# The router's keys as three products of split parts, with the splits on GpSimd

## The chip, the core and the metric

The kernel runs on one core of one Trainium2 chip. The core has five engines that run side by side, each its own list of instructions in order, and that wait for one another through semaphores: TensorE (PE, with its weight loads shown apart as PEld), VectorE (DVE), ScalarE (ACT), GpSimd (POOL) and SyncE (SP), which here issues DMAs. The metric is the device time of one execution in microseconds; a time is the median of several runs.

## The reference, cut to what matters

Thirty-two sequences of 128 tokens with 128 channels pass through a transformer block (self attention with 16 heads, cross attention to a context, a gelu MLP) and then through a block of routed experts. The change touches one product of the second block:

```python
nx = layer_norm(x, ln_gamma, ln_beta)              # 128 tokens x 128 channels, each sequence
q = nx @ Wq
k = prototype_bank @ Wk                            # prototype_bank is the context
scores = einsum('bth,bph->btp', q, k) * H ** -0.5
weights = softmax(scores)
evidence = weights @ (prototype_bank @ Wv)
combined = concat([nx, evidence, anchor])
router_probs = softmax(combined @ router_W + router_b)
h = silu(combined @ e_w1[e] + e_b1[e])             # three experts, 256 wide each
routed = sum over e of (h @ e_w2[e] + e_b2[e]) * router_probs[e]
g = sigmoid(silu(combined @ gate_w1 + gate_b1) @ gate_w2 + gate_b2)
out = x + g * (routed @ out_w + out_b)
```

## The kernel before, in words

The 32 sequences are worked in 8 groups of 4, so a group's tile is 128 partitions by 512 columns. The first 320 us or so are attention. Near their end the kernel derives matrices from the weights; one is `A`, the product of `Wk` and `Wq` (line 965, copied out of PSUM at line 779), so that the scores need one product per group, `A` with the transposed context (`keys`, line 1031), and one with the normalised tokens (`scores`).

The MLP of the 8 groups follows, and the router and experts after that. The order of the work there is written out by hand: `MLP_STEPS` (line 383) and `ROUTER_STEPS` (line 391) list steps as (name, how many groups ahead, part), and `rest_of_groups` (line 418) walks the lists. Every engine walks the same lists and emits what it has for a step, so a step's place in the list is its place in each engine's queue. Router steps of the first two groups are spread between the last MLP steps (lines 425 to 432); the first iteration over `ROUTER_STEPS` is unrolled, four run in a loop (line 446), and three more are unrolled.

An iteration of the router begins with the seven `hidden` products of group i and ends with its four `expert` products. In between stand the steps for the two groups ahead: statistics and normalisation, keys, transposition, scores and softmax for group i+2, and the evidence of group i+1.

Names that the prediction uses:

- `keys`: TensorE multiplies `A` with `CTXT`, the transposed context of one group, both float32, into a PSUM bank; VectorE copies the bank to `KEYS` (line 869).
- `hidden`: six products per chunk, of operands that are split in two parts of type float32r, the value rounded (high) and what rounding left (low): high by high, high by low, low by high, for the tokens (`NXS` with `WNS`) and for the evidence (`EVS` with `US`).
- `split` (line 663) is the GpSimd helper that makes such parts: one tensor-tensor instruction adds zeros to the source and writes the high part, and after a semaphore a second one subtracts that from the source and writes the low part. It runs for `EVS` (step `evidence`) and for `NXS` (step `nx_read`).
- `expert` for each of four sequences: TensorE makes three products side by side; VectorE adds the bias (`T`, line 933), multiplies the first third by its probability (`R`, line 936), and adds the other two in two more instructions (line 939, each waits for the one before it). TensorE has two banks for this, so the product for sequence b waits until VectorE has read that for b-2 (line 1089).
- Between expert 0 and expert 1 VectorE has the steps `scores` (lines 880 to 887) and `gate` (line 926).
- `stats` and `norm` are row statistics and normalisation (lines 814 to 828), with the inverse deviation from GpSimd (lines 655, 657).
- SyncE loads a group's context (`CTX`) and transposed context (`CTXT`, one buffer for all groups); the load of `CTXT` waits for the keys of the group before (line 631).

Of the kernel before, what the change touches and what calls it, by code (L numbers as in the profile page):

```python
# [25 lines left out]
P = 128  # L26
# [187 lines left out]
def round_steps(i):  # L214
    if i == -1:
        steps = first_steps()
    elif i == 0:
        steps = [e for e in regular_steps(0) if e[2] not in ("xt_s", "proj_s", "yt_s", "v1")]
        steps += (fill_steps(0.2, "xt_s", 2, (0, 0.3), (1, 2.1))
                  + stats_steps(3.2, 4.2, "ln_s", 3) + norm_steps(5.0, "ln_s", 3)  # L220
                  + fill_steps(14.0, "xt_s", 3, (0, 14.1), (1, 15.1))
                  + fill_steps(27.0, "proj_s", 0, (0, 27.1), (1, 27.2)) + fill_steps(30.0, "yt_s", 0, (1, 30.1))
                  + [(20.1, "load", "weights", 0, 0)])
    elif i in (1, 2):
        steps = [e for e in regular_steps(i) if i == 2 or e[2] not in ("proj_s", "yt_s")]
        steps += (fill_steps(10.0, "proj_s", 2 * i - 1, (0, 10.1), (1, 10.2))
                  + fill_steps(12.0, "yt_s", 2 * i - 1, (1, 12.1)))
        if i == 1:
            steps += (fill_steps(27.0, "proj_s", 2, (0, 27.1), (1, 27.2)) + fill_steps(30.0, "yt_s", 2, (1, 30.1))
                      + [(4.1, "load", "weights", 1, 0), (20.1, "load", "weights", 2, 0)])  # L230
    elif i == NG - 3:
        steps = (crossed_steps(i) + early_statistics(i) + fill_steps(27.0, "proj_s", NG - 1, (0, 27.1), (1, 27.2))
                 + fill_steps(30.0, "yt_s", NG - 1, (1, 30.1)))
    elif i == NG - 2:
        steps = (crossed_steps(i) + fill_steps(27.0, "proj_c", NG - 4, (1, 27.1))
                 + fill_steps(29.0, "yt_c", NG - 4, (1, 29.1)))
    elif i == NG - 1:
        steps = (fill_steps(3.0, "v1", i, (1, 3.1))
                 + fill_steps(8.0, "proj_c", NG - 3, (1, 8.1)) + fill_steps(10.0, "yt_c", NG - 3, (1, 10.1))
                 + fill_steps(12.0, "derive", 0, (0, 12.1), (1, 12.1), (2, 12.2))  # L240
                 + fill_steps(15.0, "derive", 1, (0, 15.1)) + fill_steps(17.0, "derive", 2, (0, 17.1))
                 + fill_steps(19.0, "derive", 3, (0, 19.1)) + fill_steps(21.0, "derive", 4, (0, 21.1))
                 + fill_steps(23.0, "derive", 5, (0, 23.1)) + fill_steps(25.0, "derive", 6, (0, 25.1))
                 + fill_steps(27.0, "proj_c", NG - 2, (1, 27.1)) + fill_steps(29.0, "yt_c", NG - 2, (1, 29.1))
                 + fill_steps(31.0, "mlp_xt", 0, (0, 31.1))
                 + [(t, "split", "weights", k, 0) for k, t in enumerate((2.5, 6.0, 9.0, 22.5, 24.5))]
                 + mlp_steps(21.2, "stats", 0) + mlp_steps(23.4, "norm", 0)
                 + mlp_steps(25.5, "stats", 1))
    elif i == NG:
        steps = (mlp_steps(0.2, "norm", 1)  # L250
                 + mlp_steps(2.0, "first", 0, 0) + mlp_steps(2.1, "first", 0, 1) + mlp_steps(2.6, "stats", 2)
                 + mlp_steps(3.0, "xt", 1) + mlp_steps(5.0, "first", 0, 2) + mlp_steps(5.1, "xt_read", 1)
                 + mlp_steps(7.0, "first", 0, 3) + mlp_steps(8.0, "gelu", 0, 2) + mlp_steps(8.01, "second", 0, 0)
                 + fill_steps(8.1, "proj_c", NG - 1, (1, 8.11)) + mlp_steps(8.2, "second", 0, 1)
                 + mlp_steps(8.21, "gelu", 0, 3) + mlp_steps(8.22, "norm", 2) + mlp_steps(8.23, "xt", 2)
                 + fill_steps(8.3, "yt_c", NG - 1, (1, 8.31)) + mlp_steps(8.32, "stats", 3)
                 + mlp_steps(8.4, "first", 1, 0) + mlp_steps(8.41, "second", 0, 2) + mlp_steps(8.42, "first", 1, 1)
                 + mlp_steps(8.43, "second", 0, 3) + mlp_steps(8.44, "norm", 3) + mlp_steps(8.45, "first", 1, 2)
                 + mlp_steps(8.46, "first", 1, 3) + mlp_steps(8.35, "xt_read", 2) + mlp_steps(8.36, "xt_parts", 2) + mlp_steps(5.11, "xt_parts", 1) + mlp_steps(8.48, "gelu", 1, 2)
                 + mlp_steps(8.49, "gelu", 1, 3) + mlp_steps(8.5, "gate", 0))  # L260
    elif i == NG - 4:
        steps = regular_steps(i) + early_statistics(i)
    else:
        steps = regular_steps(i)
    return sorted(e for e in steps if 0 <= e[3] < NG)
# [58 lines left out]
def attention_events(i):  # L324
# [64 lines left out]


ROUTER_STEPS = (
    ("probs", 0, 0), ("weigh", 1, 0),
    ("hidden", 0, 0),
    ("hidden", 0, 1), ("stats", 2, 0),
    ("hidden", 0, 2), ("keys", 2, 0), ("norm", 2, 0),
# [22 lines left out]
def rest_of_groups(eng, mlp, router, before_router=lambda: None, before_expert=lambda: None):  # L418

    for step in valid_steps(ROUTER_STEPS, -3):  # L420
        router(*step)
    for i in range(3, NG - 3):
        for step in valid_steps(MLP_STEPS, i):
            mlp(*step)
    lead, second = valid_steps(ROUTER_STEPS, -2), valid_steps(ROUTER_STEPS, -1)
    for i, b in ((NG - 3, lead[0:2]), (NG - 2, lead[2:]), (NG - 1, second[:-2])):
        a = valid_steps(MLP_STEPS, i)
        for at in range(max(len(a), len(b))):
            for step in a[len(a) * at // max(len(a), len(b)):len(a) * (at + 1) // max(len(a), len(b))]:
                mlp(*step)  # L430
            for step in b[len(b) * at // max(len(a), len(b)):len(b) * (at + 1) // max(len(a), len(b))]:
                router(*step)
    for step in second[-2:]:
        router(*step)
    for step in valid_steps(MLP_STEPS, NG):
        mlp(*step)
    before_router()
    for step in valid_steps(ROUTER_STEPS, 0):
        if step[0] == "hidden" and step[2] == 2:
            for last in valid_steps(MLP_STEPS, NG + 1):  # L440
                mlp(*last)
        if step[0] == "expert" and step[2] == 0:
            before_expert()
        router(*step)
    pairs = (NG - 3 - 1) // 2
    with eng.Fori(0, pairs) as j:
        for t in range(1, 3):
            for name, lag, k in ROUTER_STEPS:
                router(name, 2 * j + (t + lag), k, (t + lag) % 2, j + (t + lag) // 2)
    for i in range(1 + 2 * pairs, NG):  # L450
        for step in valid_steps(ROUTER_STEPS, i):
            router(*step)


def later(g):

    return not isinstance(g, int) or g > 0


def mlp_and_router(nc, stack, X, V, ctxin, ctxtin, w, vec, rows1, condT, mod, gbm, half, zeros, YT, ident, PS, load_w2, out,  # L460
# [72 lines left out]
    D = rb("r_D", [P, GT])  # L533
    W1S = rb("m_W1S", [P, 2, 4 * P], F32R)
    XTS = [rb(f"m_XTS{k}", [P, 2, GT], F32R) for k in range(2)]

    reused.close()
    attended = bank_read["yt_c"]
# [21 lines left out]
    xt_high, xt_split = high_ready["k0"], low_ready["k0"]  # L560
    masked = sem("masked")
    ctx_in = [sem(f"ctx_in{k}") for k in range(2)]
    keys_done = sem("keys_done")
    keys_read = sem("keys_read")
    nx_turned = sem("nx_turned")
# [57 lines left out]
    def sync_programs(sp):  # L623
        def body(name, g, k, par, pair):
            if name == "load":
# [2 lines left out]
                sp.dma_start(CTX[par][:, :, :], ctxin[bass.ds(g * GB, GB)].rearrange("b p h -> p b h"))\  # L628
                    .then_inc(ctx_in[par], 16)
                if later(g):  # L630
                    sp.wait_ge(keys_done, g)
                sp.dma_start(CTXT[:, :].rearrange("h (b p) -> h b p", b=GB),
                             ctxtin[bass.ds(g * GB, GB)].rearrange("b h p -> h b p")).then_inc(ctx_in[par], 16)
            elif name == "finish":
# [11 lines left out]
    def gpsimd_programs(pool):  # L646
# [23 lines left out]
        def router(name, g, k, par, pair):  # L670
            if name == "stats":
                inverse_deviation(1, g)
            elif name == "nx_read":
                pool.wait_ge(nx_read, g + 1)
                if not isinstance(g, int) or g > 1:
# [6 lines left out]
                split(EVS[par], EV[par][:, :], (ev_high, g + 1), ev_split)  # L682

        def split_weights(k):
            lo = (0, GT, 0, 0, GT)[k]
            hi = min(lo + GT, NHC * P)
            if k == 0:
                pool.wait_ge(load_w2, 80)
            elif k == 2:

                pool.wait_ge(shifted_done, 16 * (2 * NG - 2))
                return split(W1S, w("mlp1"), (weights_high, k + 1), weights_split)
            elif k > 2:
                pool.wait_ge(bank_read["derive"], DERIVED.index(("u_low", "u_high")[k - 3]) + 1)
            to, source = (WNS, w("e_nx", lo, hi - lo)) if k < 2 else (US, U[:, lo:hi])
            split(to[:, :, lo:hi], source, (weights_high, k + 1), weights_split)
# [259 lines left out]
    def tensor_programs(pe):  # L956
# [68 lines left out]

        def router(name, g, k, par, pair):
            if name == "keys":
                pe.wait_ge(ctx_in[par], 32 * (pair + 1))
                if later(g):
                    pe.wait_ge(nx_read, g)  # L1030
                product(EVIDENCE_BANK[:, :], A[:, :], CTXT[:, :]).then_inc(keys_done, 1)
            elif name == "nx_turn":
                pe.wait_ge(d_norm[1], g + 1)
                pe.wait_ge(keys_read, g + 1)
# [73 lines left out]

        def before_router():

            pe.wait_ge(weights_split, 2 * -(-NHC * P // GT) + 1)
            pe.wait_ge(xt_read, NG)
            pe.wait_ge(gelu_done, 4 * NG)

# [873 lines left out]
```

## Time and profile before

| what | value |
|---|---|
| median of 3 runs | 562.56 us (562.55 to 564.73) |
| the profiled execution's own time | 563.06 us |
| its span, first to last instruction | 561.2 us |
| busy: PE, PEld, DVE, ACT, POOL | 94%, 68%, 77%, 68%, 49% |
| mean granted TensorE clock | 0.991 of full speed |
| chain that ended last, by engine | PE 63%, DVE 15%, POOL 7%, DMA 5%, issue 4%, ACT 4% |
| POOL busy in 411 to 432 us, one iteration of the router | 5.77 of 21 us |
| DVE busy in the same stretch | 15.96 of 21 us |
| PE busy in the same stretch | 20.94 of 21 us |

Busy shares are averages; a PE that is busy all the time in this view may still wait, since matmuls are pipelined and their ends are modelled. The chain that ended last is followed backwards from the last instruction, at each step to what released it; a piece of another engine in the middle of PE's pieces is a place where PE had to wait for that engine.

### The profile page before, as it was taken

To read this page: it belongs to the slowest core of one execution; us is meant where nothing else is said; L and a number is where in the kernel's file an instruction comes from. 1 tells how busy PE (TensorE), PEld (TensorE's weight loads), DVE (VectorE), ACT (ScalarE), POOL (GpSimd) and SP (SyncE) were. 2 spreads that over 40 slices of the span, in tenths; PEclk is the share of its full clock that TensorE was granted. 3 is DMA by queue.
4 is the path that set the end of the run, shared out by engine and by line. 5 is a ranking of instruction groups with operands and counts; after the bars stand their busy time and mean duration, and the time that the engine had idled before them with its cause. 6 is when DMAs were issued, how large, how long until landed. Compare 5 with 4: busy or idle time off the path is not lost.

```text
span 561.2 us, 16447 instructions
## 1 busy us (share of the span) xinstructions
PE 529.0 (94%) x6175; PEld 384.4 (68%) x6177; DVE 433.5 (77%) x1271; ACT 380.5 (68%) x889; POOL 276.2 (49%) x296
## 2 busy tenths in 40 slices
PE   6988999999999999999999989998999999999995
PEld 5745666666566665666676756665788788888885
DVE  4778889788989889888887667767586786786565
ACT  6537778587787886878787685555754864864862
POOL 5637849569498686888860413224124124124100
PEclk9989999899999999999999999999999999999998
DMA  4665635634254343543330001001011011010000
GB/s 133 153 181 137 179 100 151 139 94 106 61 137 120 79 125 81 132 117 100 82 79 4 2 23 36 1 20 37 3 39 56 23 35 56 23 38 14 20 20 19
DMA packets 52939, 41.47 MB, mean 74 GB/s; under 512 B 6369, under 2 KB 52226, under 8 KB 52866
## 3 DMA queue, kind: packets, MB, share of 16 engines
q1 hardware_dynamic: 50792, 36.72, 24.9%
q10 hardware_dynamic: 2074, 3.77, 2.4%
q8 instruction: 47, 0.77, 0.6%
q14 instruction: 26, 0.21, 0.1%
HBM read 12.16 MB, written 2.10 MB: 25 GB/s over the span
## 4 chain that ended last, share of the span: by engine, by line
PE 63%; DVE 15%; POOL 7%; DMA 5%; issue 4%; ACT 4%; SPq 2%; ACTq 0%; DVEq 0%; POOLq 0%
PE PS L958 31%; PE PS L1833 7%; PE PS L1799 5%; PE PS L1885 4%; DVE NM L1613 3%; PE PS L1897 3%; PE PS L994 2%; DMA Qs<-MT 2%; PE PS L1817 2%; PE PS L1855 2%; PE PS L1890 2%; SPq L1343 2%; DVE r_T L933 2%; DVE r_R L936 1%; PE PS L1877 1%
## 5 line engine op out<-in xcount | busy, mean ns | idle before, releaser
L1613 DVE TENSOR_REDUCE NM<-PS 128x4 f32<-128x512 f32 x256 | 163.3, 681 | 30.0 <-PE PS L1799 29.4
L1499 ACT ACTIVATE PR<-PS 128x512 f32<-128x512 f32 x256 | 139.7, 600 | 27.0 <-PE PS L1817 26.4
L1799 PEld LDWEIGHTS PS<-Ks,Qs 64*128 64x128 bf16 x1024 | 57.3, 94 | 53.8 <-DVE NM L1613 28.7
L1799 PE MATMUL PS<-Ks,Qs 64*128 64x128 bf16 x1024 | 83.4, 218 | 5.6 <-DVE NM L1613 3.8
L1817 PE MATMUL PS<-Qs,Ks 64*128 64x128 bf16 x1024 | 83.6, 218 | 3.9 <-DMA Qs<-MT 3.3
L1833 PE MATMUL PS<-PR,Va 128*32 128x128 f32 x2048 | 83.3, 281 | 0.0
L744 ACT ACTIVATE r_HID<-PS,ANC 128x128 f32<-128x128 f32 x224 | 62.4, 378 | 18.5 <-PE PS L958 18.5
L655 POOL TENSOR_TENSOR m_veps<-m_mv,m_eps 128x4 f32<-128x4 f32 x16 | 3.6, 225 | 129.7 <-DVE m_mv L820 129.7
L1833 PEld LDWEIGHTS PS<-PR,Va 128*32 128x32 f32 x2048 | 48.5, 110 | 20.2 <-ACT PR L1499 6.9
L1817 PEld LDWEIGHTS PS<-Qs,Ks 64*128 64x128 bf16 x1024 | 57.1, 94 | 7.5 <-DMA Qs<-MT 3.8
L958 PE MATMUL PS<-r_NXS,r_WNS 128*128 128x512 f32 x168 | 52.6, 421 | 0.0
L958 PE MATMUL PS<-WO,r_HID 128*128 128x128 f32 x384 | 47.7, 278 | 0.5
L958 PE MATMUL PS<-r_EVS,r_US 128*128 128x512 f32 x168 | 47.6, 391 | 0.0
L958 PEld LDWEIGHTS PS<-WO,r_HID 128*128 128x128 f32 x384 | 44.6, 192 | 2.0 <-DVE r_T L933 1.7
L1885 PE MATMUL PS<-XT,W 128*128 128x512 f32 x64 | 35.9, 648 | 1.7 <-ACT XT L1535 1.4
L724 ACT ACTIVATE m_H<-PS,V 128x512 f32<-128x512 f32 x32 | 21.9, 688 | 21.7 <-PE PS L958 21.5
L958 PEld LDWEIGHTS PS<-r_EVS,r_US 128*128 128x128 f32 x168 | 31.5, 188 | 7.2
L958 PEld LDWEIGHTS PS<-r_NXS,r_WNS 128*128 128x128 f32 x168 | 29.9, 189 | 8.2 <-issue 3.4
L958 PE MATMUL PS<-m_XTS,m_W1S 128*128 128x512 f32 x96 | 30.7, 442 | 1.9 <-DVE m_XTS L847 1.5
L770 ACT ACTIVATE r_GTH<-r_GS 128x512 f32<-128x512 f32 x8 | 5.0, 630 | 39.1 <-DVE r_GS L926 39.1
L958 PE MATMUL PS<-m_H,W 128*128 128x512 f32 x64 | 31.5, 592 | 0.0
L1386 POOL TENSOR_TENSOR veps<-mv,eps 128x4 f32<-128x4 f32 x24 | 4.8, 201 | 49.4 <-DVE mv L1678 49.4
(198 smaller groups left out, 1110.1 us busy)
## 6 DMA issues: line engine op xcount, KB each, us to landing
Qs<-Qp SPq DMA_DIRECT2D x96, 128.0 KB
Ks<-Kp SPq DMA_DIRECT2D x90, 128.0 KB
CTXG<-in_ctx SPq DMA_DIRECT2D x8, 256.0 KB, 3.9
r_CTX<-in_ctx SPq DMA_DIRECT2D x8, 256.0 KB, 2.9
r_CTXT<-in_ctxt SPq DMA_DIRECT2D x8, 256.0 KB, 3.3
out<-X SPq DMA_DIRECT2D x8, 256.0 KB, 2.3
X<-in_x SPq DMA_DIRECT2D x7, 256.0 KB, 4.5
W<-in_weights ACTq DMA_DIRECT2D x2, 855.0 KB
```

What stands on the lines that cost most here:

```text
L724: nc.scalar.activation(H[:, k, :], FIRST_BANK[k % 2][:, :], ACT.Gelu_apprx_tanh, bias=vec("bmlp1", k))\
L744: last = nc.scalar.activation(HID[:, k, b * P:(b + 1) * P], HIDDEN_BANK[k % 3][:, b * P:(b + 1) * P], ACT.Silu, bias=ANC[:, k, bass.ds(g * ...
L933: nc.vector.tensor_tensor(t, EXPERT_BANK[b % 2][:, 0:NE * P], BO[:, 0:NE * P], ALU.add)\
L958: return nc.tensor.matmul(to, lhsT, rhs, start=start, stop=stop)
L994: last = nc.tensor.transpose(bank[:, b * P:(b + 1) * P], source(b), ident[:, :])
L1499: nc.scalar.activation(PR[:, u, :], T_BANK[u % 2][:, :], ACT.Exp, scale=SCALE)\
L1613: nc.vector.tensor_reduce(out=NM[:, c.b // 2, c.second, u // 2, u % 2 * 4:u % 2 * 4 + 4, 0], in_=S_BANK[score_bank(c, u)[0]][:, :].rearran ...
L1799: last = nc.tensor.matmul(S_BANK[bank][:, j * P:(j + 1) * P], Qs[c.stack][rows, lo + j, cols], Ks[c.stack][rows, lo + j, cols], start=True ...
L1817: last = nc.tensor.matmul(T_BANK[u % 2][:, j * P:(j + 1) * P], Ks[c.stack][rows, lo + j, cols], Qs[c.stack][rows, lo + j, cols], start=Tru ...
L1833: last = nc.tensor.matmul(O_BANK[p.turn][TW * j:TW * j + TW, at:at + P], Va[c.mem][:, c.b, 4 * (u // 2) + j, u % 2 * TW // 2:u % 2 * TW // ...
L1885: last = nc.tensor.matmul(PS[fill_bank(name, g)][:, :], w(WEIGHT[name[0]][kind]), source(name, g)[:, :], start=True, stop=True)
L1897: last = nc.tensor.matmul(GROUP_BANK[:, :], w(("proj", "cproj")[KIND[name]]), OgT[KIND[name]][:, :], start=True, stop=True)
```

## The change

The keys become three products of split parts, like the hidden products. Two tiles are new: `AS`, the two parts of `A`, made once by GpSimd in the last round of attention (a sixth `split` of weights), and `CTXS`, the two parts of `CTXT`, made by GpSimd for each group in a new router step, `ctx_parts`. It stands near the start of an iteration, two groups ahead. It waits for the context's DMAs and, since `CTXS` is one buffer, for the keys of the group before; the keys wait for it, and the next load of `CTXT` now waits for it instead of for the keys.

```diff
-                 + [(t, "split", "weights", k, 0) for k, t in enumerate((2.5, 6.0, 9.0, 22.5, 24.5))]
+                 + [(t, "split", "weights", k, 0) for k, t in enumerate((2.5, 6.0, 9.0, 22.5, 24.5, 26.5))]
...
 ROUTER_STEPS = (
-    ("probs", 0, 0), ("weigh", 1, 0),
+    ("probs", 0, 0), ("weigh", 1, 0), ("ctx_parts", 2, 0),
     ("hidden", 0, 0),
...
-    for i, b in ((NG - 3, lead[0:2]), (NG - 2, lead[2:]), (NG - 1, second[:-2])):
+    for i, b in ((NG - 3, lead[0:3]), (NG - 2, lead[3:]), (NG - 1, second[:-2])):
...
+    AS = rb("r_AS", [P, 2, P], F32R)
+    CTXS = rb("r_CTXS", [P, 2, GT], F32R)
...
                 if later(g):
-                    sp.wait_ge(keys_done, g)
+                    sp.wait_ge(ctx_split, g)
                 sp.dma_start(CTXT[:, :].rearrange("h (b p) -> h b p", b=GB),
...
+            elif name == "ctx_parts":
+                pool.wait_ge(ctx_in[par], 32 * (pair + 1))
+                if later(g):
+                    pool.wait_ge(keys_done, g)
+                split(CTXS, CTXT[:, :], (ctx_high, g + 1), ctx_split)
...
+            elif k == 5:
+                pool.wait_ge(bank_read["derive"], 1)
+                return split(AS, A[:, :], (weights_high, k + 1), weights_split)
...
             if name == "keys":
-                pe.wait_ge(ctx_in[par], 32 * (pair + 1))
+                pe.wait_ge(ctx_split, g + 1)
                 if later(g):
                     pe.wait_ge(nx_read, g)
-                product(EVIDENCE_BANK[:, :], A[:, :], CTXT[:, :]).then_inc(keys_done, 1)
+                else:
+                    pe.wait_ge(weights_split, 6)
+                product(EVIDENCE_BANK[:, :], AS[:, 0, :], CTXS[:, 0, :], True, False)
+                product(EVIDENCE_BANK[:, :], AS[:, 0, :], CTXS[:, 1, :], False, False)
+                product(EVIDENCE_BANK[:, :], AS[:, 1, :], CTXS[:, 0, :], False, True).then_inc(keys_done, 1)
```

In GpSimd's queue the first half of the router's loop stood like this before: the statistics, the split of the evidence, the split of the tokens, and then the next iteration's statistics.

```order
L666 TENSOR_TENSOR r_EVS<-r_EV,zeros 128x512
L668 TENSOR_TENSOR r_EVS<-r_EV,r_EVS 128x512
L676 ISA
L666 TENSOR_TENSOR r_NXS<-r_NX,zeros 128x512
L668 TENSOR_TENSOR r_NXS<-r_NX,r_NXS 128x512
L654 REGISTER_ALU
L655 TENSOR_TENSOR m_veps<-m_mv,m_eps 128x4
L657 TENSOR_TENSOR m_rstd<-m_veps,half 128x4
```

And the same place in GpSimd's queue now (line numbers of the changed kernel):

```order
L670 TENSOR_TENSOR r_EVS<-r_EV,zeros 128x512
L672 TENSOR_TENSOR r_EVS<-r_EV,r_EVS 128x512
L685 ISA
L670 TENSOR_TENSOR r_NXS<-r_NX,zeros 128x512
L672 TENSOR_TENSOR r_NXS<-r_NX,r_NXS 128x512
L678 ISA
L670 TENSOR_TENSOR r_CTXS<-r_CTXT,zeros 128x512
L671 REGISTER_ALU
L672 TENSOR_TENSOR r_CTXS<-r_CTXT,r_CTXS 128x512
L659 TENSOR_TENSOR m_veps<-m_mv,m_eps 128x4
L661 TENSOR_TENSOR m_rstd<-m_veps,half 128x4
```

The two instructions of the context's split follow the token split of the iteration before, with only their waits in between.

The step also changes how the router steps of the first group are spread between the MLP steps. VectorE's queue there, before (`X<-PS,X` adds an MLP result; the four `BN_STATS` after it are the router's statistics of group 0):

```order
L860 TENSOR_TENSOR X<-PS,X 128x512
L814 BN_STATS m_stat<-X 128x6 x4
L818 COPY seen<-m_stat 128x1
L820 BN_AGGR m_mv<-m_stat 128x2 x4
L828 SCALAR_TENSOR_TENSOR m_XN<-X,m_mv,m_rstd 128x128 x4
L854 TENSOR_SCALAR YT<-PS,mod,gbm 128x128 x4
L869 COPY KEYS<-PS 128x4x128
```

The same place in VectorE's queue now:

```order
L872 TENSOR_TENSOR X<-PS,X 128x512
L840 SCALAR_TENSOR_TENSOR m_XN<-X,m_mv,m_rstd 128x128 x4
L826 BN_STATS m_stat<-X 128x6 x4
L830 COPY seen<-m_stat 128x1
L832 BN_AGGR m_mv<-m_stat 128x2 x4
L866 TENSOR_SCALAR YT<-PS,mod,gbm 128x128 x4
L881 COPY KEYS<-PS 128x4x128
```

The last MLP normalisation (`m_XN`) has moved ahead of the router's first statistics.

## Rows read from the trace of the kernel before

**Rows 1.** Chain of waits, 400 to 470 us: start us, us, what.

```profile
432.29 0.36 DVE r_R L939
...
434.56 0.56 DVE r_T L933
...
435.16 9.35 PE PS L958 x44
```

**Rows 2.** Timeline, 424 to 446 us, POOL: start us, us, engine, line, op, tiles, [idle before].

```profile
429.71 1.04 POOL L666 TENSOR_TENSOR r_NXS<-r_NX,zeros 128x512 fp32r<-128x512 f32 x1
430.83 1.27 POOL L668 TENSOR_TENSOR r_NXS<-r_NX,r_NXS 128x512 fp32r<-128x512 f32 x1
...
443.67 0.20 POOL L655 TENSOR_TENSOR m_veps<-m_mv,m_eps 128x4 f32<-128x4 f32 x1 [11.57 <-DVE m_mv L820]
```

**Rows 3.** Timeline, 428 to 437 us, DVE.

```profile
431.17 1.08 DVE L936 TENSOR_TENSOR r_R<-r_T,r_RP 128x128 f32<-128x128 f32 x1
432.29 0.74 DVE L939 SCALAR_TENSOR_TENSOR r_R<-r_T,r_RP,r_R 128x128 f32<-128x128 f32 x2
...
435.14 0.29 DVE L936 TENSOR_TENSOR r_R<-r_T,r_RP 128x128 f32<-128x128 f32 x1
```

**Rows 4.** Timeline, 312.9 to 317.4 us, POOL: the split of a weight matrix.

```profile
312.94 1.04 POOL L666 TENSOR_TENSOR r_US<-U,zeros 128x512 fp32r<-128x512 f32 x1
314.06 1.27 POOL L668 TENSOR_TENSOR r_US<-U,r_US 128x512 fp32r<-128x512 f32 x1
315.28 0.87 POOL L666 TENSOR_TENSOR r_US<-U,zeros 128x384 fp32r<-128x384 f32 x1
```

**Rows 5.** Timelines of narrow windows, 312.9 to 317.5 us, DVE: one normalisation's four instructions.

```profile
313.00 1.12 DVE L828 SCALAR_TENSOR_TENSOR m_XN<-X,m_mv,m_rstd 128x128 f32<-128x128 f32 x1 [1.41 <-POOL m_rstd L657]
314.05 1.42 DVE L828 SCALAR_TENSOR_TENSOR m_XN<-X,m_mv,m_rstd 128x128 f32<-128x128 f32 x1
315.40 1.98 DVE L828 SCALAR_TENSOR_TENSOR m_XN<-X,m_mv,m_rstd 128x128 f32<-128x128 f32 x2
```

**Rows 6.** Timelines, 365 to 370 and 427 to 447 us, PE.

```profile
367.22 1.02 PE L958 MATMUL PS<-r_CTXT,A 128*128 128x512 f32 x2
368.08 0.60 PE L994 MATMUL PS<-ident,m_XN 128*128 128x128 f32 x4
...
440.04 0.84 PE L958 MATMUL PS<-r_EVS,r_US 128*128 128x512 f32 x3
440.72 1.02 PE L958 MATMUL PS<-r_CTXT,A 128*128 128x512 f32 x2
```

**Rows 7.** Loads of the transposed context: timeline of SP, and times by tile.

```profile
427.53 0.39 SPq L632 DMA_DIRECT2D r_CTXT<-in_ctxt  x1
...
DMA to landing us min/median/max: 2.6/3.3/4.6
```

**Rows 8.** Timeline, 360 to 386 us, DVE: the router's first groups between the MLP's last.

```profile
364.92 0.86 DVE L814 BATCH_NORM_STATS2 m_stat<-X 128x6 f32<-128x128 f32 x4
...
366.17 1.11 DVE L828 SCALAR_TENSOR_TENSOR m_XN<-X,m_mv,m_rstd 128x128 f32<-128x128 f32 x4
...
367.43 1.36 DVE L854 TENSOR_SCALAR YT<-PS,mod,gbm 128x128 f32<-128x128 f32 x4
...
370.25 0.43 DVE L845 CAST m_XTS<-m_XT 128x512 fp32r<-128x512 f32 x1 [0.87 <-ACT m_XT L736]
...
378.14 0.17 DVE L887 TENSOR_SCALAR r_nbias<-r_nmax 128x4 f32<-128x4 f32 x1
```

**Rows 9.** The same stretch, POOL.

```profile
363.39 1.46 POOL L657 TENSOR_TENSOR m_rstd<-m_veps,half 128x4 f32<-128x4 f32 x1
...
375.22 1.26 POOL L668 TENSOR_TENSOR r_NXS<-r_NX,r_NXS 128x512 fp32r<-128x512 f32 x1
```

**Rows 10.** Chain of waits, 355 to 400 us.

```profile
372.52 0.65 PE PS L994 x4
...
377.07 1.28 ACT L752
```

More of the change, by code:

```diff
@@ L562, in mlp_and_router @@
     ctx_in = [sem(f"ctx_in{k}") for k in range(2)]
+    ctx_high = sem("ctx_high")
+    ctx_split = sem("ctx_split")
     keys_done = sem("keys_done")
@@ L684, in split_weights @@
         def split_weights(k):
-            lo = (0, GT, 0, 0, GT)[k]
+            lo = (0, GT, 0, 0, GT, 0)[k]
             hi = min(lo + GT, NHC * P)
@@ L1109, in before_router @@
         def before_router():
-            pe.wait_ge(weights_split, 2 * -(-NHC * P // GT) + 1)
+            pe.wait_ge(weights_split, 2 * -(-NHC * P // GT) + 2)
             pe.wait_ge(xt_read, NG)
```

## The prediction

> **What bounds the kernel now.** I read the busy shares first, then the chain of waits in the stage of the change, then the timelines of VectorE and GpSimd beside each other. By the shares, TensorE is the bound of the router's stage and GpSimd has room. The chain says more. In each iteration of the router it leaves TensorE for one stretch: it goes through VectorE's work on expert 0 (`r_R`), through the scores and gate steps, to the reading of expert 1's product (`r_T`), which ends at 435.12, and only then back to TensorE, whose products of expert 3 start at 435.16 [rows 1]. TensorE waits there for VectorE's reading of the product two sequences back. The same pieces stand in the chain six times (line 939's begin at 411, 432, 453, 474, 495 and 516 us). So in the expert phase VectorE is the bound, and a delay of VectorE between 431 and 435 us delays TensorE one for one; the steps behind it (the softmax on ScalarE, the next hidden products) all hang on the same two engines and shift with them.
>
> GpSimd is idle from 432.10, when the token split ends, for 11.57 us until the next statistics [rows 2]. In front of that idle stretch stands a collision that is already there: the first multiplication `r_R` takes 1.08 us where it takes 0.29 us elsewhere [rows 3]. It starts at 431.17, during the split's second instruction (430.83 to 432.10) [rows 2], and ends at 432.25, 0.15 us after that instruction. It reads two SBUF tiles, and the split reads SBUF too.
>
> How a whole run of such instructions fares, a stretch of the attention's last round shows. Four instructions of a normalisation, which read two SBUF tiles each, meet a split of four GpSimd instructions. The first ends at 314.12 and the second at 315.47 [rows 5], each 0.14 us after GpSimd's first (312.94 + 1.04 = 313.98) and second (314.06 + 1.27 = 315.33) [rows 4]; all four end at 317.38 after 4.38 us, where the like takes 1.11 us undisturbed [rows 8]. GpSimd's own times are those of an undisturbed split (1.04 and 1.27 us, as in rows 2). So one VectorE instruction gets through after each GpSimd instruction, and the 0.08 us between a split's two halves (313.98 to 314.06) is too short for a second.
>
> **The change, part by part.** The sum is made against the profiled execution (span 561.2 us, its own time 563.06 us, 0.5 us above the median of 562.56 us); I add the difference to the median.
>
> *The context's split in the expert phase.* Its wait for the context is over in time: the load is issued at 427.53, and with the median landing of 3.3 us is there at 430.8, with the longest of 4.6 us at 432.13 [rows 7]. The wait for the keys of the group before is long met. So the split follows the token split at once; the third instruction of rows 4 starts 0.05 us before the second one ends, so here the first half, call it A, starts at about 432.05 and ends at 433.1. VectorE's `r_R` was waiting earlier and ends at 432.25 as before. The first of the two instructions of line 939 starts at 432.29, inside A, and ends 0.14 us after it, at 433.24, instead of 432.65. The second half B starts 0.08 us after A, at 433.18, before line 939's second instruction, which must wait for the first's result; B ends at 434.45 (1.27 us) and that second instruction at 434.59. Before, the two were done at 432.29 + 0.74 = 433.03 [rows 3]. Shift: 1.56 us. What follows on VectorE up to the reading of expert 1 reads PSUM and at most one SBUF tile, and B is over by then; so expert 3 starts 1.56 us later. The split of group g+1 follows the token split of group g for groups 3 to 7, which are five expert phases (411, 432, 453, 474 and 495 us). 5 x 1.56 = +7.8 us. Bounds: nothing, if the split finds the gaps, and 5 x 1.95 = +9.8 us, if `r_R` too loses its turn to A (rivals below).
>
> *The splits of groups 0, 1 and 2.* That of group 0 lies behind the MLP statistics that end at 363.39 + 1.46 = 364.85 [rows 9]: A from 364.8 to 365.85, B from 365.93 to 367.2. VectorE now has the last MLP normalisation first, where the router's statistics began at 364.92 [rows 8]. Its four instructions end at 0.14 us behind A and B for the first two, and about 0.27 us each for the rest: 367.87. The statistics, 366.17 - 364.92 = 1.25 us, end at 369.1, and the gate step, which began at 367.43, begins there, 1.7 us later. VectorE idled 0.87 us before the cast at 370.25, so the rest comes 0.8 us later, and the transposition at 372.52, which hangs on it in the chain [rows 10], too: +0.8 us, between 0 (if later waits swallow it) and 1.7. The split of group 1 runs behind the token split that ended at 375.22 + 1.26 = 376.48 [rows 9], now about 0.8 us later; its second half would be at work from 378.4 to 379.65, while VectorE's one small instruction of line 887 (378.14 [rows 8], now 378.95) has one SBUF input. Behind that stands ScalarE's exponential, on the chain directly after its table load [rows 10]. No row shows such an instruction beside a split. It costs 0 if it passes, and 0.6 us if it waits for B; I take +0.3, the middle, since neither end has a nearer row. The split of group 2 meets no VectorE work with two SBUF inputs: 0.
>
> The Trainium skill (SBUF — State Buffer, "Who interferes with whom") says that VectorE and GpSimd share one pair of SBUF ports, that an instruction of VectorE with two SBUF inputs blocks against a GpSimd instruction that reads SBUF, and that a tensor-scalar instruction can block as well, when it runs in a mode that uses both ports. By that last rule the small instruction would wait and the term be 0.6 instead of 0.3; no run here shows it.
>
> *The products.* With one float32 product per group the next work of TensorE starts 0.86 us after the keys (367.22 to 368.08); three products of float32r parts take 0.68 us from start to start (440.04 to 440.72) [rows 6]. Saved: 0.18 us per group. In six groups (2 to 7) TensorE is in the chain at the keys: -1.1 us. For groups 0 and 1 the chain runs through VectorE and ScalarE at that time, and nothing is gained.
>
> *The split of `A`*, two instructions on 128 columns, falls into the last round of attention, where GpSimd waits for statistics; no VectorE work there has two SBUF inputs, and its reader is some 45 us off: 0. The moved wait of SyncE (on the split instead of the keys) is met earlier than the old one: 0; its queue holds the output's store behind it, which does not come later by it.
>
> Sum: +7.8 + 0.8 + 0.3 - 1.1 = +7.8 us; 563.06 + 7.8 = 570.9 for a profiled execution, and 562.56 + 7.8 = 570.4 us for the median.
>
> **Rivals.** *The split stays hidden.* GpSimd has 11.57 us of room and the split needs 2.4 us; if A starts after about 432.7, when line 939's second instruction has read its tiles, nothing collides until 435.14, and there only what is left of B. The point that decides is the start of A: 0.65 us later than I have it. For it: a wait on a DMA and one on TensorE, and in every second iteration the loop's branch, stand before A, and the longest landing is at 432.13. Against it: the median landing leaves 1.2 us, and the token split itself begins with no gap behind the evidence split. Then -1.1 us: 561.5 us, not slower.
>
> *Only the first half collides*: line 939's second instruction gets ahead of B and ends at 433.24 + 0.04 + 0.35 = 433.63. Shift 0.6, five times 3.0; with the other terms +3.0: 565.6 us. Against it stands rows 5, where no second instruction got into such a gap, though there it did not have to wait for a result and was earlier.
>
> *Three collisions*: A takes its turn before the waiting `r_R`. Then `r_R` ends at 433.24, line 939's first at 434.59 and its second at 434.98: 1.95 us, five times 9.8; +9.8: 572.4 us. Against it: at 315.28 a split's next instruction started behind a waiting one of VectorE, which ended only 0.14 us after the instruction before [rows 4, 5].
>
> The same page of the Trainium skill says that issue order decides which of two blocks the other; by that, too, the waiting `r_R` comes first and the third rival falls.
>
> **How the numbers follow.** Both halves collide: 0.72; only the first: 0.11; hidden: 0.09; three: 0.06; something that makes it faster than the saved 1.1 us: 0.02. A measurement of this kernel can tell 0.5% from no change, 2.8 us. The forecast's own range, by the bounds of the lead terms (0 to 1.7, 0 to 0.6) and 0.2 us on each of five shifts, is 568.5 to 572.3. The range for 8 in 10 takes in part of the case with one collision and the one with three: 565.0 to 572.9. Slower by over 0.5%: the forecast, the third rival and over half of the second, 0.85; within 0.5%: the hidden case and the rest, 0.13; faster: 0.02.
>
> **What will show it.** In five expert phases the first instruction of line 939 should take about 0.95 us and the second about 1.3, each ending about 0.14 us after a half of the context's split, and TensorE's wait before expert 3 should grow by about 1.6 us; an iteration of the loop should be some 1.4 us longer. The keys should take 0.68 us to the next product. The iterations from 516 us on should be as before. The prediction is wrong if line 939's two instructions keep their 0.74 us, or if TensorE finds other work's end behind which the wait hides.

## The result, and the profile after

The changed kernel takes 570.88 us (median of 4 runs, 570.64 to 577.5) against 563.17 us for the kernel before (4 runs, 562.55 to 564.73): a ratio of 1.0161 with a 95% interval of 1.0085 to 1.0238, so it is slower, by something between 0.9% and 2.4%. The forecast was 570.4 us. The execution profiled took 570.64 us with a span of 568.8 us, at a mean granted clock of 0.991, the same as before.

The page of the changed kernel first: the busy times, the chain that ended last by engine, and one row of the costliest groups. Line numbers from the router on are 12 higher than before (line 939 is now 951, line 933 is 945).

```profile
PE 527.8 (93%) x6183; PEld 385.9 (68%) x6185; DVE 443.7 (78%) x1271; ACT 380.9 (67%) x889; POOL 295.9 (52%) x314
...
PE 56%; DVE 18%; POOL 8%; DMA 5%; issue 5%; SPq 4%; ACT 3%; ACTq 0%; DVEq 0%; POOLq 0%
...
L951 DVE SCALAR_TENSOR_TENSOR r_R<-r_T,r_RP,r_R 128x128 f32<-128x128 f32 x64 | 30.6, 478 | 2.3
```

The busy shares hardly say what happened: TensorE fell from 94% to 93% and GpSimd rose from 49% to 52%. The chain does: TensorE's part went from 63% to 56%, VectorE's from 15% to 18%, and line 951, two instructions per sequence, has come up among the costliest groups with a mean of 478 ns. Now the place. GpSimd's timeline of the changed kernel, 428 to 437 us:

```profile
432.59 1.27 POOL L672 TENSOR_TENSOR r_NXS<-r_NX,r_NXS 128x512 fp32r<-128x512 f32 x1
433.82 1.09 POOL L670 TENSOR_TENSOR r_CTXS<-r_CTXT,zeros 128x512 fp32r<-128x512 f32 x1
434.99 1.27 POOL L672 TENSOR_TENSOR r_CTXS<-r_CTXT,r_CTXS 128x512 fp32r<-128x512 f32 x1
```

VectorE beside it, from timelines of narrow windows (434 to 434.5 and 435.2 to 435.9 us), which show line 951's two instructions apart:

```profile
432.91 1.10 DVE L948 TENSOR_TENSOR r_R<-r_T,r_RP 128x128 f32<-128x128 f32 x1
434.05 1.01 DVE L951 SCALAR_TENSOR_TENSOR r_R<-r_T,r_RP,r_R 128x128 f32<-128x128 f32 x1
435.09 1.31 DVE L951 SCALAR_TENSOR_TENSOR r_R<-r_T,r_RP,r_R 128x128 f32<-128x128 f32 x1
```

Three VectorE instructions in a row end behind three of GpSimd: 434.01 behind 433.86, 435.06 behind 434.91, 436.40 behind 436.26, which is 0.14 to 0.15 us each time. Before, only the first did, and the other two took 0.74 us together [rows 3]. The chain of waits, 360 to 475 us, of the changed kernel:

```profile
432.32 0.57 DVE r_T L945
432.91 1.11 DVE r_R L948
434.05 1.02 DVE r_R L951
...
437.94 0.56 DVE r_T L945
438.54 9.13 PE PS L970 x45
...
454.73 0.57 DVE r_T L945
```

and two lines of the same chain of the kernel before, which bound the same iteration there:

```profile
430.58 0.57 DVE r_T L933
...
451.57 0.57 DVE r_T L933
```

The reading of expert 0's product starts an iteration of the router in this count: 454.73 - 432.32 = 22.41 us now and 451.57 - 430.58 = 20.99 us before. From it to the reading of expert 1's product are 437.94 - 432.32 = 5.62 us, where there were 434.56 - 430.58 = 3.98 us [rows 1]. TensorE takes up expert 3 at 438.54, directly behind, as it did at 435.16 before [rows 1]. What its weight loads waited for in 400 to 540 us, in total, times and the longest, shows that it lost this time, in the changed kernel:

```profile
PEld PS L970 <- DVE r_T L945: 9.8, 6, 2.0
```

and in the kernel before:

```profile
PEld PS L958 <- DVE r_T L933: 1.7, 6, 0.3
```

The products went as forecast. TensorE's timeline of the changed kernel, 440 to 447 us, shows the three products of the keys between the hidden ones:

```profile
443.40 0.85 PE L970 MATMUL PS<-r_EVS,r_US 128*128 128x512 f32 x3
444.09 0.85 PE L970 MATMUL PS<-r_CTXS,r_AS 128*128 128x512 f32 x3
444.77 0.85 PE L970 MATMUL PS<-r_NXS,r_WNS 128*128 128x512 f32 x3
```

From the keys to the next product are 0.68 us, the same as for any hidden chunk, instead of 0.86 us for the float32 product [rows 6].

The lead phase has the two small terms. VectorE's timelines of the changed kernel, 363 to 371 and 376 to 383 us:

```profile
363.66 0.69 DVE L872 TENSOR_TENSOR X<-PS,X 128x512 f32<-128x512 f32 x1 [0.33 <-PE PS L1006]
364.27 2.96 DVE L840 SCALAR_TENSOR_TENSOR m_XN<-X,m_mv,m_rstd 128x128 f32<-128x128 f32 x4
...
378.14 0.71 DVE L899 TENSOR_SCALAR r_nbias<-r_nmax 128x4 f32<-128x4 f32 x1
```

and GpSimd in the same stretch, the second halves of the splits of groups 0 and 1:

```profile
365.29 1.27 POOL L672 TENSOR_TENSOR r_CTXS<-r_CTXT,r_CTXS 128x512 fp32r<-128x512 f32 x1
...
377.55 1.28 POOL L672 TENSOR_TENSOR r_CTXS<-r_CTXT,r_CTXS 128x512 fp32r<-128x512 f32 x1
```

The normalisation takes 2.96 us instead of 1.11 [rows 8]. The small instruction takes 0.71 us instead of 0.17 [rows 8]; it ends at 378.85, 0.02 us behind GpSimd's 378.83, and ScalarE, which was ready for the exponential, waits for it (ACT's timeline, 376 to 383 us):

```profile
378.88 0.37 ACT L764 ACTIVATE r_E<-PS,r_nbias 128x128 f32<-128x128 f32 x1 [0.52 <-DVE r_nbias L899]
```

### The profile page after: what moved, and what is told of

The parts are those of the page before. It is cut to its first block, busy times and chain, and to the rows that moved or that the text cites. A ratio compares the mean times of both kernels' runs of the same rounds, so it can differ in the third digit from the quotient of the medians.

```text
span 568.8 us, 16491 instructions
## 1 busy us (share of the span) xinstructions
PE 527.8 (93%) x6183; PEld 385.9 (68%) x6185; DVE 443.7 (78%) x1271; ACT 380.9 (67%) x889; POOL 295.9 (52%) x314
## 4 chain that ended last, share of the span: by engine, by line
PE 56%; DVE 18%; POOL 8%; DMA 5%; issue 5%; SPq 4%; ACT 3%; ACTq 0%; DVEq 0%; POOLq 0%
PE PS L970 28%; PE PS L1849 6%; PE PS L1815 5%; DVE NM L1629 3%; PE PS L1901 3%; SPq L1359 3%; PE PS L1006 2%; PE PS L1913 2%; DMA Qs<-MT 2%; PE PS L1833 2%; DVE r_R L951 2%; PE PS L1871 2%; DVE r_T L945 2%; PE PS L1906 2%; DVE r_R L948 1%
## 5 line engine op out<-in xcount | busy, mean ns | idle before, releaser
L970 PE MATMUL PS<-r_NXS,r_WNS 128*128 128x512 f32 x168 | 50.0, 406 | 0.0
L951 DVE SCALAR_TENSOR_TENSOR r_R<-r_T,r_RP,r_R 128x128 f32<-128x128 f32 x64 | 30.6, 478 | 2.3
```

The lines of the kernel that those rows point to most:

```text
L951: nc.vector.scalar_tensor_tensor(R[:, b, :], t[:, e * P:(e + 1) * P], RP[:, b, e:e + 1], R[:, b, :], ALU.mult, ALU.add).then_inc(routed, 1)
L970: return nc.tensor.matmul(to, lhsT, rhs, start=start, stop=stop)
```

## Experiments

The theory: VectorE's instructions that read two SBUF tiles wait for each GpSimd instruction that reads SBUF (here tiles of 128x512), and in the expert phase they stand on the path that sets the end. Rivals: the three products with their new operands and waits cost the time; any activity of GpSimd there does, writing too; or the loss is in the queue and would follow the split wherever it is put.

The total times of one kernel vary by some us, mostly from the attention stage: the aggregation of the fourth MLP group's statistics (line 820) begins at 334.2 us in one profile here and at 339.0 in another. An iteration of the router repeats within 0.05 us (the sixth takes 19.70 to 19.74 us in the six kernels whose sixth nothing touches). So I compare lengths of iterations, from one reading of expert 0's product to the next, beside the ratios:

| kernel | iterations 1 to 6, us | us, median | ratio to before, 95% |
|---|---|---|---|
| before | 20.87 21.00 20.90 21.01 20.85 19.71 | 562.77 to 564.07 in three batches | 1 |
| after | 22.26 22.41 22.45 22.41 22.29 19.74 | 570.88 | 1.0161 (1.0085 to 1.0238) |
| split, old product | 22.43 22.63 22.53 22.61 22.43 19.70 | 571.45 | 1.0125 (1.0060 to 1.0191) |
| writes alone | 20.66 20.79 20.75 20.82 20.67 19.71 | 563.21 | 0.9979 (0.9945 to 1.0013) |
| context split later | 20.79 20.97 21.03 20.97 20.96 19.72 | 565.16 | 1.0025 (0.9990 to 1.0060) |
| before, token split later | 20.55 20.58 20.59 20.61 20.47 19.21 | 562.31 | 0.9967 (0.9930 to 1.0003) |
| context split earlier | 20.70 20.88 21.05 20.99 20.85 19.71 | 562.42 | 0.9998 (0.9972 to 1.0023) |
| both moved | 20.42 20.38 20.44 20.41 20.28 19.24 | 558.69 | 0.9917 (0.9882 to 0.9951) |

**The split with the old product.** The changed kernel, with the keys made by one float32 product again; GpSimd still splits the context, and nobody uses the parts. The next load of `CTXT` waits for the keys again, too, since they read it.

```diff
                     sp.wait_ge(ctx_split, g)
+                    sp.wait_ge(keys_done, g)
...
-                product(EVIDENCE_BANK[:, :], AS[:, 0, :], CTXS[:, 0, :], True, False)
-                product(EVIDENCE_BANK[:, :], AS[:, 0, :], CTXS[:, 1, :], False, False)
-                product(EVIDENCE_BANK[:, :], AS[:, 1, :], CTXS[:, 0, :], False, True).then_inc(keys_done, 1)
+                product(EVIDENCE_BANK[:, :], A[:, :], CTXT[:, :]).then_inc(keys_done, 1)
```

> The changed kernel with the old keys: GpSimd still splits each group's context at the same place, and nobody reads the parts; TensorE makes the one float32 product of before. Theory (the split collides with VectorE's multiplications of expert 0, and the new products save a little): all of the loss stays and the saving goes, 5 x 1.6 for the expert phases, 0.6 and 0.5 for the first two groups, so 563.2 + 9.2 = 572.4 us, 571.0 to 573.5; line 951's first two instructions of five expert phases take about 1.0 and 1.3 us. Rival (the three products and their waits cost TensorE the time): back to 563 us.

Measured: 571.45 us (4 runs, 570.68 to 572.05). The iterations are 1.56 to 1.63 us longer than before and 0.08 to 0.22 us longer than with the three products. VectorE's timeline of this kernel, 432 to 438 us, has the collision unchanged (its lines 949 and 952 are 948 and 951 of the changed kernel):

```profile
432.83 1.08 DVE L949 TENSOR_TENSOR r_R<-r_T,r_RP 128x128 f32<-128x128 f32 x1
433.95 2.35 DVE L952 SCALAR_TENSOR_TENSOR r_R<-r_T,r_RP,r_R 128x128 f32<-128x128 f32 x2
```

As forecast, the loss is the split's, all of it, and the products save a little; the first rival falls.

**Writes alone.** The changed kernel, where from group 1 on two fills of the parts with zeros, with a tiny sum ahead of them, take the place of the split: GpSimd writes the same tiles and reads almost nothing. The keys of these groups are made of zeros. A fill takes 0.52 us where a half of the split takes 1.04 or 1.27.

```diff
                 if later(g):
                     pool.wait_ge(keys_done, g)
+                if later(g):
+                    pool.wait_ge(ctx_high, g)
+                    nc.gpsimd.tensor_tensor(tiny[:, :], half[:, :], half[:, :], ALU.add).then_inc(ctx_high, 1)
+                    nc.gpsimd.memset(CTXS[:, 0, :].bitcast(F32), 0.0).then_inc(ctx_split, 1)
+                    return nc.gpsimd.memset(CTXS[:, 1, :].bitcast(F32), 0.0).then_inc(ctx_split, 1)
                 split(CTXS, CTXT[:, :], (ctx_high, g + 1), ctx_split)
...
```

> The changed kernel, but from group 1 on GpSimd fills the two parts of the context with zeros at the same place in its queue (a tiny sum and two memsets that only write, some 0.45 us each) instead of splitting the context; the keys of these groups are then made of zeros. Theory (what collides is a GpSimd instruction that reads SBUF with a VectorE instruction that reads two SBUF tiles): the multiplications of expert 0 take their undisturbed 0.35 us each although GpSimd is at work beside them, and the time is 563.2 + 0.6 (group 0, still split) - 1.2 (products) = 562.6 us, 561.5 to 563.5. Rival (any GpSimd work beside VectorE's delays it, by as much as it lasts): about 0.5 us or more in each of five expert phases, 565 to 567 us.

Measured: 563.21 us (12 runs, 560.52 to 566.97); the iterations are 0.15 to 0.21 us shorter than before, the products' gain. In one of the five expert phases (430 us) the tiny sum waited for the context's load, and the fills came behind line 957's instructions (line 951 of the changed kernel). In the other four they lie on top of them. GpSimd's timeline of this kernel, 405 to 420 us:

```profile
411.66 0.25 POOL L684 TENSOR_TENSOR r_tiny<-half 128x4 f32<-128x4 f32 x1
411.84 0.52 POOL L685 MEMSET r_CTXS<- 128x512 f32 x1
412.30 0.52 POOL L686 MEMSET r_CTXS<- 128x512 f32 x1
```

and VectorE's, 411 to 413.3 us:

```profile
411.88 0.74 DVE L957 SCALAR_TENSOR_TENSOR r_R<-r_T,r_RP,r_R 128x128 f32<-128x128 f32 x2
```

The two instructions keep their 0.74 us (411.88 to 412.62) under two fills (411.84 to 412.82). Writing on GpSimd does not hold them up, and the split, which reads as well, does: the second rival falls. The Trainium skill (SBUF — State Buffer, "Who interferes with whom") says just that: two SBUF inputs contend with a GpSimd instruction that reads SBUF, not with one that only writes.

**The context's split later.** The changed kernel with one wait more, from group 3 on: the split waits until expert 0's three multiplications are done.

```diff
             elif name == "ctx_parts":
...
+                if not isinstance(g, int) or g > 2:
+                    pool.wait_ge(routed, NE * GB * (g - 3) + NE)
                 split(CTXS, CTXT[:, :], (ctx_high, g + 1), ctx_split)
```

> The changed kernel with one more wait: from group 3 on the context's split waits until VectorE's three multiplications of expert 0 are done. Theory (the loss is a matter of where the split stands, and decided by VectorE's way to the reading of expert 1): line 951 is undisturbed at expert 0; the split then runs beside the scores and gate steps, which read PSUM, with only the small single-input instruction of line 899 (0.2 to 0.3 us) in its way, and ends beside the multiplication of expert 1, which is off TensorE's way. TensorE's wait before expert 3 falls from 2.0 to about 0.6 us: 570.9 - 5 x 1.3 = 564.4 us, 563.0 to 565.5. Rival (VectorE has no slack anywhere, so a later collision costs the same): 569 to 571 us.

Measured: 565.16 us (12 runs, 563.3 to 570.42), iterations within 0.13 us of those before. GpSimd's timeline of this kernel, 428 to 440 us, and VectorE's, 431 to 438 us:

```profile
433.93 1.04 POOL L670 TENSOR_TENSOR r_CTXS<-r_CTXT,zeros 128x512 fp32r<-128x512 f32 x1 [1.00 <-DVE r_R L953]
```

```profile
433.11 0.74 DVE L953 SCALAR_TENSOR_TENSOR r_R<-r_T,r_RP,r_R 128x128 f32<-128x128 f32 x2
...
434.69 0.30 DVE L901 TENSOR_SCALAR r_nbias<-r_nmax 128x4 f32<-128x4 f32 x1
```

The same split 1 us later in the same queue costs almost nothing, so the third rival falls: line 953 (951 of the changed kernel) is back at 0.74 us. What is left is 0.13 us from the small instruction (0.30 instead of 0.17 us; it ends at 434.99, 0.02 behind the split's first half), and it eats most of what the products save.

**The kernel before, with its token split later.** The collision that was there already [rows 3] should be worth removing by itself. One wait is added, of the same kind, ahead of the token split from group 2 on.

```diff
+                if not isinstance(g, int) or g > 1:
+                    pool.wait_ge(routed, NE * GB * (g - 2) + NE)
                 split(NXS[par], NX[par][:, :], (nx_high, g + 1), nx_split)
```

> The kernel before with one more wait: from group 2 on GpSimd's split of the normalised tokens waits until VectorE's three multiplications of expert 0 are done, so that the collision that the kernel before already has (0.7 to 0.8 us on the first multiplication in six or seven expert phases) goes. Theory (it lies on the chain until TensorE's own work is the bound): TensorE's wait of 0.3 us before expert 3 goes in seven phases, 563.2 - 2.2 = 561.0 us, 560.0 to 562.2. Rival (VectorE's way is not what holds expert 3): no change, 563.2 us.

Measured: 562.31 us (12 runs, 558.82 to 566.92). GpSimd's timeline of this kernel, 432 to 441 us, and VectorE's, 433 to 440 us:

```profile
435.74 1.04 POOL L666 TENSOR_TENSOR r_NXS<-r_NX,zeros 128x512 fp32r<-128x512 f32 x1 [2.54 <-DVE r_R L941]
```

```profile
434.60 0.29 DVE L938 TENSOR_TENSOR r_R<-r_T,r_RP 128x128 f32<-128x128 f32 x1
434.92 0.74 DVE L941 SCALAR_TENSOR_TENSOR r_R<-r_T,r_RP,r_R 128x128 f32<-128x128 f32 x2
...
437.89 0.39 DVE L938 TENSOR_TENSOR r_R<-r_T,r_RP 128x128 f32<-128x128 f32 x1
```

The first multiplication (line 938, line 936 of the kernel before) is at 0.29 us, and expert 1's product is read 437.32 - 434.00 = 3.32 us behind expert 0's, 0.66 less than before. What the later split now meets is cheap: expert 1's first multiplication takes 0.39 us instead of 0.29. The five iterations from the first on are shorter by 0.31 to 0.42 us only: TensorE no longer waits for VectorE there, so its own work is the bound and the rest is not to be had. In the view of its weight loads' waits in 400 to 540 us, `r_T` no longer stands at all, for 1.7 us before. With 0.50 us in the sixth, the iterations are 2.3 us shorter together, as the theory had it (2.2). The median misses its range, 560.0 to 562.2 us, by 0.1 us, and the interval of the ratio still takes in 1.

**The context's split earlier.** The changed kernel, with the step moved one group further ahead, behind the normalisation, where GpSimd is idle; `CTXT` is loaded ahead of `CTX` and has a semaphore of its own.

```diff
-    ("probs", 0, 0), ("weigh", 1, 0), ("ctx_parts", 2, 0),
+    ("probs", 0, 0), ("weigh", 1, 0),
...
-    ("hidden", 0, 2), ("keys", 2, 0), ("norm", 2, 0),
+    ("hidden", 0, 2), ("keys", 2, 0), ("norm", 2, 0), ("ctx_parts", 3, 0),
...
-                pool.wait_ge(ctx_in[par], 32 * (pair + 1))
+                pool.wait_ge(ctxt_in, 16 * (g + 1))
                 if later(g):
                     pool.wait_ge(keys_done, g)
+                    pool.wait_ge(d_norm[1], g)
...
```

> The changed kernel with the context's split moved to where VectorE has no instruction with two SBUF inputs: one group further ahead, behind the router's normalisation (from group 1 on it waits for the normalisation of the group before; that of group 0 runs between two MLP normalisations), with the load of the transposed context in front of that of the context, so that it lands an iteration earlier. Theory: no collision is left at expert 0 beyond that of the token split, an iteration of the loop takes 20.7 us (0.2 less than the kernel before, the saving of the products), the small instruction of line 899 keeps 0.17 us, and the time is some 1.2 us below the kernel before. Rival (the split costs by being on GpSimd at all, or the split of the evidence, which now stands behind it, comes late for the next hidden products): an iteration of 21.5 us or more.

Measured: 562.42 us (12 runs, 559.45 to 564.46); the iterations are those of before within 0.17 us, not 0.2 us shorter, and the median is 0.3 us below that of the kernel before, not 1.2: a miss. GpSimd's timeline of this kernel, 443 to 456 us:

```profile
445.49 1.04 POOL L676 TENSOR_TENSOR r_CTXS<-r_CTXT,zeros 128x512 fp32r<-128x512 f32 x1 [1.35 <-DVE r_XN L849]
446.61 1.29 POOL L678 TENSOR_TENSOR r_CTXS<-r_CTXT,r_CTXS 128x512 fp32r<-128x512 f32 x1
...
451.31 1.26 POOL L678 TENSOR_TENSOR r_NXS<-r_NX,r_NXS 128x512 fp32r<-128x512 f32 x1
```

and VectorE's, of the narrow window 451.4 to 452 us:

```profile
451.11 0.29 DVE L957 TENSOR_TENSOR r_R<-r_T,r_RP 128x128 f32<-128x128 f32 x1
451.44 1.28 DVE L960 SCALAR_TENSOR_TENSOR r_R<-r_T,r_RP,r_R 128x128 f32<-128x128 f32 x1
```

From 445.49 to 452.57 GpSimd now works without a gap, and the token split ends later against VectorE. Line 960 is line 951 of the changed kernel. The token split's second half meets its first instruction (which ends at 452.72, 0.15 us behind it) where it met `r_R`: a loss of 0.93 us (1.28 instead of 0.35) in place of the 0.8 us of [rows 3], which swallows the products' gain. I had moved one split and not followed the one queued behind it.

**Both moved.** The kernel of the last experiment, with the token split waiting as in the one before that: no split is left beside expert 0's multiplications.

> The version before this one in the list (context's split behind the normalisation) with the token split, too, waiting for the three multiplications of expert 0, as in the run that moved that split in the kernel before. Theory: both effects add, since they are in different places: 0.2 from the products and 0.36 from TensorE's wait before expert 3, an iteration of 20.35 us, and in all 3.5 us below the kernel before. Rival (with the wait before expert 3 gone, TensorE waits for something else, the transposition of the weights or the keys' copy, and the gains overlap): an iteration of 20.6 us.

Measured: 558.69 us (10 runs, 555.23 to 566.27), 0.9917 (0.9882 to 0.9951): faster than both kernels. The theory's iteration of 20.35 us came (20.28 to 20.44 in the first five), the rival's 20.6 did not. Its chain of waits, 400 to 460 us:

```profile
406.48 15.61 PE PS L981 x105
422.08 0.61 PE PS L1017 x4
422.70 3.83 PE PS L981 x20
426.53 0.44 PE PS L1017 x4
426.97 15.56 PE PS L981 x105
```

There is nothing but TensorE in it; the stretch of VectorE that cut each iteration [rows 1] is gone. GpSimd's timeline of this kernel, 424 to 440 us, and VectorE's, 428 to 436 us:

```profile
430.97 1.04 POOL L676 TENSOR_TENSOR r_NXS<-r_NX,zeros 128x512 fp32r<-128x512 f32 x1 [2.13 <-DVE r_R L962]
```

```profile
429.83 0.29 DVE L959 TENSOR_TENSOR r_R<-r_T,r_RP 128x128 f32<-128x128 f32 x1
430.15 0.74 DVE L962 SCALAR_TENSOR_TENSOR r_R<-r_T,r_RP,r_R 128x128 f32<-128x128 f32 x2
```

The first six iterations together are 121.16 us (408.82 to 529.98) instead of 124.33 (409.71 to 534.04). The products' saving counts here (the first five are 0.13 to 0.20 us shorter than in the kernel before with its token split later), because TensorE is the bound. Not all of the gain comes from the splits: the profiled spans differ by 4.0 us (557.2 and 561.2), the six iterations by 3.2. The transpositions of groups 0 and 1 are 13.49 us apart in this kernel and in the last one, where they were 14.22. The moved step in the list has put one of the MLP's products (three matmuls with `m_XTS`) ahead of group 0's transposition, at a place where TensorE had waited 0.28 us for VectorE. No run takes this 0.7 us apart from the rest.

## Why the prediction was right, by its steps

- *The context's split beside expert 0.* Forecast 1.56 us in each of five phases; measured, from the reading of expert 0's product to that of expert 1's, 1.61 to 1.64 us, five times, 8.1 us for a forecast of 7.8. The 0.06 us is GpSimd's: the first half started at 433.82, in the forecast's place, but took 1.09 us and not 1.04, and the second half 0.05 us later with it. Both instructions of line 951 came out 1.01 and 1.31 us for a forecast of 0.95 and 1.3, and the 0.14 us behind each half held. The step on what gets through (one VectorE instruction after each GpSimd one, the waiting one first) is what the rows show: `r_R` ended at 434.01, before the first half did. So the third rival, where it loses its turn, did not come, and neither did the one where only the first half collides. The load of the context was there in time in all five phases (no idle time ahead of the first half), so the hidden case did not come either. Its deciding point was sound: in the experiment with the later start the split begins 433.93 - 431.40 = 2.53 us behind the reading of expert 0's product, where it began at 433.82 - 432.32 = 1.50, and the 8 us are gone. Its price was 1 us too good in the iterations, because the small instruction behind is then held up, and its 561.5 us left out the two lead terms, +0.8 and +0.3 us, which stay in that case.
- *Group 0.* Forecast +0.8. From the last MLP sum (`X<-PS,X`) to the transposition are 372.50 - 363.66 = 8.84 us now; before, with the sum at 364.31 in that trace and the transposition at 372.52 [rows 10], 8.21: +0.63. The normalisation ended where I had it: 3.57 us behind the start of that sum (364.27 + 2.96 - 363.66), forecast 367.87 - 364.31 = 3.56. The 0.2 us less came out behind it, where VectorE's queue up to the cast ran a little closer than the forecast's whole durations end to end. In the kernels with the split between MLP normalisations (the last two experiments) the step is 0.1 us.
- *Group 1.* Forecast +0.3, the middle of 0 and 0.6. Measured 0.54 on the instruction. The transpositions of groups 0 and 1 are 14.75 us apart (372.50 to 387.25) and were 14.22 (372.52 to 386.74): +0.53, all of it on the path. The upper bound, 0.6 us for an instruction that waits for the split's second half, was the better value; the middle of two bounds was no evidence. The Trainium skill (SBUF — State Buffer, "Who interferes with whom") says that a tensor-scalar instruction can contend with GpSimd as well, in a mode that uses both ports; the wait agrees with that, but no run shows the mode.
- *The products.* Forecast -1.1 in six groups. The iterations grew by 1.39 to 1.55 us where their expert phases grew by 1.61 to 1.64, so five groups saved about 0.95 us together, and the sixth 0.16 (from group 1's transposition to expert 0's first reading, 22.81 us for 22.97): -1.1.
- *The split of `A`, the moved wait of SyncE, and the iterations from 516 us on*: nothing, as forecast; the sixth iteration is 19.74 us for 19.71.

The sum of the measured terms is 8.1 + 0.63 + 0.53 - 1.1 = +8.2 us; the stage up to the statistics of the fourth MLP group was 0.65 us shorter in this execution (334.60 us for 335.25), within what that stage varies, and the span grew by 7.6 us (561.2 to 568.8). The terms that were off, +0.3, -0.2 and +0.2, are smaller than this variation. So the mechanism is right in each phase, but that the medians differ by 7.7 us, within 0.1 of the forecast, is partly luck. The prediction's own range is added up a little too narrow: its bounds give 568.3 to 572.6 us, not 568.5 to 572.3; the measured time lies in either.

## What to carry to other kernels

Room on an engine is not room at a place: GpSimd was idle for 11.57 us and the split of 2.4 us still cost 8 us, because it stood beside VectorE work with two SBUF inputs on the path that sets the end; 1 us later behind that work it cost almost nothing there. Put an operation that reads SBUF on GpSimd where VectorE reads PSUM or idles, by a wait on the work that it must not meet, and then follow every split queued behind it as well. A kernel whose chain leaves the bounding engine for another one may hide the same collision already; here taking both collisions out made a change that lost 1.6% into one that gains 0.8%, of which about 0.1% is the moved MLP product.

## What the runs showed of the hardware

A VectorE instruction with one small SBUF input is held up by GpSimd too: the tensor-scalar of 128x4 took 0.71 us for 0.17 when it came 0.69 us before a half's end, and 0.30 us when it came 0.28 us before one, and ended 0.02 us behind it each time, where those with two inputs end 0.14 to 0.15 us behind. GpSimd itself loses almost nothing in these meetings: a half of 1.04 us took 1.09.

How much GpSimd reads matters: an instruction that reads and writes only 128x4 did not hold up VectorE. In the kernel before, the four instructions of a normalisation, each with two SBUF inputs (366.17 to 367.28 us), took 1.11 us [rows 8] although two of them started while this one was at work; the router's four at 371.33, where GpSimd was idle, took 1.13 (GpSimd's timeline, 365.5 to 368 us):

```profile
366.63 1.01 POOL L657 TENSOR_TENSOR m_rstd<-m_veps,half 128x4 f32<-128x4 f32 x1
```
